# Mixtures of experts computed for the chosen pairs only, in blocks of 128 slots by expert

## Chip, core and metric

The kernel runs on one core of one Trainium2 chip. The metric is the device time of one execution in microseconds. The core's engines are TensorE (PE in the profile, its weight loads PEld), VectorE (DVE), ScalarE (ACT), GpSimd (POOL) and SyncE (SP), which here only issues transfers.

## What is computed

Eight layers run over 8 sequences of 256 tokens with 128 channels, all in float32; after each, `x = layernorm(x + layer(x))`. Four of them are attention-like (a complex scan, causal attention, local attention over a window of 32, attention to the 16 best of the last 32 tokens). The other four are: a mixture of 8 experts with 256 hidden columns, a latent attention with a mixture of 8 experts and a shared one with 128 hidden columns, a dynamics layer with its own small experts, and a mixture of 8 experts with 342 hidden columns. Each mixture has this shape; the reference computes every expert for every token, with weights that are zero for all but two:

```
for e in range(E):
    h = silu(x @ Wg[e] + bg[e]) * (x @ W1[e] + b1[e])
    out = out + we[:, e:e + 1] * (h @ W2[e] + b2[e])
```

`we` holds for each token the weights of its two best experts. The first two mixtures have no biases.

## The kernel before

The 8 sequences are 4 chunks of 2 sequences, 512 tokens each, that is 4 tiles of 128 tokens. All four chunks are under way at once. Each goes through nine stages: A (scan), B (mixture 256), C (causal attention), D1 (latent attention), D2 (mixture 128 with the shared expert), E (local attention), F (dynamics), G (attention to the best of 32), H (mixture 342). A number in brackets is the chunk: B(0) is stage B of chunk 0.

Each engine has a generator per stage that yields after every piece of work. `interleave` runs the four chunks' generators in an order that is written out by hand, one digit (the chunk) per piece: the strings of `MERGE`, one for each engine. `BANK_OF` names in the same way the PSUM bank (8 of 128 x 512 float32) that each group of products writes. Memory regions that chunks share (`att`, `ring`, `dyn`) are handed on in the order of `TURNS`; `take` waits for the last user. Semaphores order everything else, one `Signal` per kind of event.

In a mixture, `chunk_turned` transposes the chunk to channels by tokens (`xt`), `by_token` makes the 8 logits of each token, and VectorE picks the two best (`top2`: `MAX8`, `FIND_INDEX8`, comparison with 0 to 7) and makes a dense weight per token and expert (`densify`). Then `experts` runs on each engine: for each expert and each slice of its hidden columns TensorE makes gate and up over all 512 tokens (`whole`, L450), ScalarE the silu of gate into `hid` (L1818 with bias, L1820 without), VectorE multiplies by up (L1192 with bias, L1195 without), TensorE makes the down product per tile of 128 tokens (L485) and VectorE adds it to `x` with the dense weight (L1209). SP loads each expert's weights (`load_expert`, L2338, L2332 and L2334) into a ring of 4 slots, `w_exp`; the addresses are constants and the loads wait only for their slot. Attention's transposes of probabilities stand at L525 (`turn_probs`). After each stage the norm: `statistics` and `normalise` on VectorE, and between them `power` on GpSimd (L2187, L2188). ScalarE's `table` (L1781) loads another function table where the next function needs one.

GpSimd's work is otherwise part of A (L2214, L2219) and scaling of probabilities (L2199, L2202, L2271). It issues no transfer.

Of the kernel before, what the change touches and what calls it, by code (L numbers as in the profile page):

```python
# [9 lines left out]
U32 = mybir.dt.uint32  # L10
AX_X = mybir.AxisListType.X

D = 128
# [8 lines left out]
E8 = 8  # L22
# [5 lines left out]
RING_H, RING_W = 6, 4  # L28
# [27 lines left out]
TICKS = dict(A=9, B=26, C=25, D1=26, D2=19, E=30, F=58, G=20, H=34)  # L56

TURNS = {
# [10 lines left out]
        "0000000100000011200000000003200000000000000000000231111111101000001100111111101010101010111111111111"  # L69
        "0100000111000010300000111111011000000011101010100000010111110011010101110100001012222222122102000020"  # L70
        "2222202202200202222000002022222022222202200200011111111100001112000000011122221112220000011101111122"
        "1202020012033333333233222233333300002222200220322333232300000111120000321300101011313333311111310010"
        "0133333333300222223223333322330222332323203112322111012221122322133323211111111111121333131333331131"
        "3000300000033333333331113300310333113331111111333111222333311331111113222000000000000022000202000000"
        "2222200020000011200101020220021111222111112212222222222222020022221121003333003003000003003000300322"
        "2222222222222202222222233333011311111111113111111111111131111221121211331113223322333133322222233333"
        "3333311113113333223111211111333333333333333311131333333311122213312232322222222233332333333222222222"
        "2222332232222222332322222222222222222222223333333333333333333333333333333333333333333333333333333333"
# [53 lines left out]
def previous_user(region, k, st):  # L132

    turns = TURNS[region]
    i = turns.index((k, st))
    return turns[i - 1] if i and turns[i - 1][0] != k else None


class Signal:


# [8 lines left out]


FFN = {
    "B": (8, 2, 128),
    "D2": (9, 1, 128),
    "H": (8, 3, M3),
}
# [2340 lines left out]
```

## Time and profile before

| | us |
|---|---|
| median of 3 runs (1224.92 to 1227.92) | 1227.08 |
| the profiled execution | 1226.56 |
| its span, first to last instruction | 1224.5 |
| TensorE busy | 1115.4 |
| VectorE busy | 827.1 |
| ScalarE busy | 657.6 |
| GpSimd busy | 219.1 |

The profile is of one execution. Busy time is the time in which at least one instruction of the engine runs, so for TensorE, whose products overlap, it is less than count times mean. A float32 product is recorded as two instructions, a transpose as one. Of the transfers, the profile knows when they were issued and when they landed; the granted clock is the share of full speed that TensorE had.

### The profile page before, as it was taken

How to read it: one execution, taken by the hardware profiler on the slowest of the kernel's cores; microseconds unless marked ns; L12 is line 12 of the kernel's file. 1: busy time of each engine (PE TensorE's matmuls, PEld its weight loads, DVE VectorE, ACT ScalarE, POOL GpSimd, SP SyncE). 2: the span in 40 equal slices, each digit the busy share in tenths (PEclk: the TensorE clock that was granted, in tenths of full speed). 3: DMA queues.
4: the chain of work that ended last, by engine and by line, in shares of the span. 5: the costliest groups of instructions: out<-in, count | busy, mean ns of one | idle time of the engine just before them, and what ended most of it. 6: DMA issues, size and time to landing. Idle time of an engine off the chain costs nothing.

```text
span 1224.5 us, 16730 instructions
## 1 busy us (share of the span) xinstructions
PE 1115.4 (91%) x5800; PEld 629.4 (51%) x5800; DVE 827.1 (68%) x2446; ACT 657.6 (54%) x1028; POOL 219.1 (18%) x251
## 2 busy tenths in 40 slices
PE   0799967799999999999799989999999999999996
PEld 0455544566554455554455555454464553565554
DVE  6987566489577369868486696678584774664534
ACT  0225344555756766677666575668546655542321
POOL 1312042224021214131200150005020000202000
PEclk9899989899989989997899999799999999999999
DMA  7021100121110000001001111001001010111210
GB/s 268 4 73 54 39 14 14 30 68 34 33 48 24 27 14 21 20 27 33 1 14 56 37 37 37 1 18 37 18 28 37 18 37 1 45 36 54 79 56 9
DMA packets 45394, 45.91 MB, mean 37 GB/s; under 512 B 2584, under 2 KB 44192, under 8 KB 45056
## 3 DMA queue, kind: packets, MB, share of 16 engines
q1 hardware_dynamic: 42336, 40.59, 10.9%
q10 hardware_dynamic: 2976, 4.26, 1.0%
q8 instruction: 47, 0.77, 0.2%
q14 instruction: 35, 0.29, 0.1%
HBM read 43.79 MB, written 1.05 MB: 37 GB/s over the span
## 4 chain that ended last, share of the span: by engine, by line
PE 77%; DVE 13%; ACT 4%; DMA 3%; issue 2%; POOL 1%; POOLq 0%; DVEq 0%; ACTq 0%
PE bank L450 32%; PE bank L485 13%; PE bank L757 10%; PE bank L780 5%; ACT L1781 2%; PE bank L457 2%; PE bank L525 2%; PE bank L439 2%; PE bank L747 1%; PE bank L792 1%; PE bank L668 1%; DMA xt<-x_in 1%; DVE x L1209 1%; DMA w_exp<-in_ffn 1%; PE bank L508 1%
## 5 line engine op out<-in xcount | busy, mean ns | idle before, releaser
L450 PE MATMUL bank<-xt,w_exp 128*128 128x512 f32 (+1 forms) x784 | 390.6, 629 | 19.1 <-DMA w_exp<-in_ffn 6.4
L1781 ACT ACT_TABLE_LOAD x186 | 238.6, 1283 | 70.9 <-PE bank L450 41.7
L450 PEld LDWEIGHTS bank<-xt,w_exp 128*128 128x128 f32 (+1 forms) x784 | 134.5, 190 | 193.7 <-issue 117.1
L485 PEld LDWEIGHTS bank<-w_exp,hid 128*128 128x128 f32 (+1 forms) x1568 | 189.3, 196 | 52.2 <-issue 15.8
L485 PE MATMUL bank<-w_exp,hid 128*128 128x128 f32 (+1 forms) x1568 | 199.0, 282 | 5.7 <-DVE hid L1192 4.2
L1209 DVE SCALAR_TENSOR_TENSOR x<-bank,dense,x 128x128 f32<-128x128 f32 x384 | 107.9, 343 | 119.4 <-PE bank L485 103.0
L757 PE MATMUL bank<-picked,w_dyn 128*128 128x512 f32 x320 | 142.9, 596 | 0.0
L1818 ACT ACTIVATE hid<-bank,w_cols 114x512 f32<-114x512 f32 x96 | 65.2, 687 | 114.6 <-PE bank L450 114.0
L2187 POOL TENSOR_SCALAR rstd<-mv 128x4 f32<-128x4 f32 x32 | 7.0, 218 | 552.6 <-DVE mv L1075 552.4
L1820 ACT ACTIVATE hid<-bank 128x512 f32<-128x512 f32 x100 | 57.5, 597 | 85.1 <-PE bank L450 84.7
L757 PEld LDWEIGHTS bank<-picked,w_dyn 128*128 128x128 f32 x320 | 59.1, 190 | 74.8 <-issue 74.7
L2271 POOL TENSOR_TENSOR att<-att,lsm 128x512 f32<-128x512 f32 x64 | 67.8, 1075 | 140.7 <-DVE lsm L1415 130.1
L1192 DVE SCALAR_TENSOR_TENSOR hid<-bank,w_cols,hid 114x512 f32<-114x512 f32 x96 | 70.3, 745 | 27.4 <-PE bank L450 21.1
L1195 DVE TENSOR_TENSOR hid<-bank,hid 128x512 f32<-128x512 f32 x100 | 66.7, 681 | 17.9 <-ACT hid L1820 14.6
L525 PE MATMUL bank<-w_const,att 128*128 128x128 f32 x304 | 45.2, 283 | 12.0 <-DVE hid L1195 3.6
L1844 ACT COPY att<-bank 128x512 f32<-128x512 f32 (+1 forms) x80 | 41.1, 581 | 20.9 <-PE bank L525 20.9
L525 PEld LDWEIGHTS bank<-w_const,att 128*128 128x128 f32 x304 | 35.7, 145 | 30.8 <-issue 12.7
L780 PE MATMUL bank<-xt,w_dyn 128*128 128x512 f32 (+2 forms) x96 | 49.8, 617 | 1.1 <-DVE xt L1531 1.0
L1555 DVE TENSOR_TENSOR picked<-dyn,bank 128x512 f32<-128x512 f32 x64 | 39.5, 679 | 10.3 <-PE bank L450 10.3
L2202 POOL TENSOR_TENSOR att<-att,rowsum 128x512 f32<-128x512 f32 x32 | 32.8, 1051 | 74.5 <-DVE rowsum L1250 74.5
L1793 ACT ACTIVATE xt<-bank 128x512 f32<-128x512 f32 x24 | 14.3, 594 | 58.3 <-PE bank L439 58.3
L1085 DVE TENSOR_SCALAR x<-x,mv,rstd 128x128 f32<-128x128 f32 x112 | 32.5, 353 | 14.3 <-POOL rstd L2188 14.2
(288 smaller groups left out, 1515.9 us busy)
## 6 DMA issues: line engine op xcount, KB each, us to landing
w_exp<-in_ffn SPq DMA_DIRECT2D x68, 192.0 KB, 3.2
w_exp<-in_ffn SPq DMA_DIRECT2D x32, 384.0 KB, 3.5
w_exp<-in_ffn SPq DMA_DIRECT2D x32, 342.0 KB, 3.1
w_dyn<-in_dyn ACTq DMA_DIRECT2D x1, 1636.0 KB, 12.1
w_const<-in_const SPq DMA_DIRECT2D x1, 1274.0 KB, 11.7
xt<-x_in SPq DMA_DIRECT2D x4, 256.0 KB, 15.4
out<-x ACTq DMA_DIRECT2D x4, 256.0 KB, 2.3
att<-in_stage SPq DMA_DIRECT2D x1, 512.0 KB, 5.2
```

The costliest lines, as they stand in the source:

```text
L450: nc.tensor.matmul(seqs(bk[0:rows, :]) if len(rhs.shape) == 3 else bk[0:rows, :], lhsT, rhs, start=True, stop=True).then_inc(S[k % STREAMS ...
L485: last = nc.tensor.matmul(bk[:, t * 128:(t + 1) * 128], hid[0:rows, (e * nf + f) % RING_H, t * 128:(t + 1) * 128], ffn_w(k, st, "down", e, ...
L525: last = nc.tensor.transpose(bk[:, o:o + 128], a(u)[:, i * 128:(i + 1) * 128], ident)
L757: last = nc.tensor.matmul(bk[:], part("dyn", "ex_w2")[:, h * 384 + at:h * 384 + at + 128], picked[:, 2 * h + t - 1, :], start=False, stop= ...
L780: last = nc.tensor.matmul(seqs(bk[0:rows, :]), lhs, src, start=(half == 0), stop=(half == len(use) - 1))
L1192: V.scalar_tensor_tensor(o, u, col("b1", j, rows), o, ALU.add, ALU.mult).then_inc(X.hidden.s, 1)
L1195: V.tensor_tensor(o, u, o, ALU.mult).then_inc(X.hidden.s, 1)
L1209: last = V.scalar_tensor_tensor(x[:, s, t, :], bk[:, t * 128:(t + 1) * 128], dense[:, s, t, ex:ex + 1], x[:, s, t, :], ALU.mult, ALU.add)
L1781: A.preload_act_table_set(name)
L1818: A.activation(dst, src, ACT.Silu, bias=col("bg", j, rows)).then_inc(X.silu.s, 1)
L1820: A.activation(dst, src, ACT.Silu).then_inc(X.silu.s, 1)
L2271: G.tensor_tensor(v, v, spread(lsm[:, u, row, :], 2, 64), op).then_inc(done, 1)
```

## The change

Each mixture is computed only for the 1024 pairs of token and chosen expert of a chunk. The pairs are put in order of expert, each expert's begin at a multiple of 128, and 15 blocks of 128 slots hold them in every case. The steps:

- VectorE adds the one-hot choices (`count_in`), TensorE makes counts and ranks from them with a triangle of ones (`counts`), VectorE works out each pair's slot (`place`, into `pos`) and each block's expert (`name_blocks`, into `block_expert`; in H also each block's biases, `bias_x`).
- GpSimd scatters the token rows with 8 indirect transfers of 128 rows to a buffer in device memory (`scatter`, `x_slots`, two buffers in turn). SP loads them back in groups of 3 blocks (`load_slots`), TensorE transposes each block, ScalarE copies the group (`xt_group`).
- SP reads each block's expert into a register (`expert_of`) and loads gate and up weights and down weights into two rings of 4 (`load_gu`, `load_dn`). TensorE makes gate, up and down for the block's 128 slots (`products`), ScalarE and VectorE silu and product as before on 128 columns per slice (256 in B, 384 in D2's groups).
- ScalarE copies a group's results (`y_group`), SP stores them (`store_slots`, `y_slots`), GpSimd gathers each token's two rows with 8 indirect transfers (`gather`), VectorE adds them with their two weights (`combine`). The shared expert of D2 runs over all tokens with weights of its own in place (`w_shared`).
- Before GpSimd's first work in stage A it waits for six new transfers that fill `x_slots` (twice 1921 rows of 512 bytes, from the input in device memory) and one row of each `y_slots`.
- `MERGE`, `BANK_OF` and `TURNS` are written anew, and SP has an order of its own. The mixtures share no region any more; D2(0) comes after B(3). In F, the router's first values go to `nx`, so that `dyn` is taken later. `hid` has 4 slots of 384 columns in place of 6 of 512.

The core of the diff, without the new orders:

```diff
+NB, GROUP = 15, 3
+GROUPS = NB // GROUP
+MIX = {"B": (2, 128), "D2": (1, 128), "H": (3, M3)}
...
+            def counts(k, st):
+                bk = begin(k, (st, "counts"), (T.placed, (k, st, "read")))
+                pe.wait_ge(T.placed.s, T.placed.at(k, st, "counted"))
+                nc.tensor.matmul(bk[:, 0:40], part("const", "ones"), routing(s)[:, 40:80], start=True, stop=False)
+                nc.tensor.matmul(bk[:, 8:40], tri[:], routing(s)[:, 0:32], start=False, stop=True).then_inc(T.filled, 1)
...
+            def products(k, st, u, half, bk, at):
+                nf, rows = MIX[st]
+                for n, j in enumerate(blocks_of(st, u)):
+                    if half == 0:
+                        pe.wait_ge(*gu_landing(k, st, j))
+                    g = j // GROUP
+                    for f in range(nf):
+                        o = at + (n * nf + f) * 128
+                        c = (j % GROUP) * 128
+                        last = nc.tensor.matmul(bk[0:rows, o:o + 128], w_gate_up(k, st, j, half, f),
+                                                xt_group[:, group_slot(k, st, g), c:c + 128], start=True, stop=True)
+                return last
...
-                    for t in range(TILES):
-                        for f in range(nf):
-                            last = nc.tensor.matmul(bk[:, t * 128:(t + 1) * 128],
-                                                    hid[0:rows, (e * nf + f) % RING_H, t * 128:(t + 1) * 128],
-                                                    ffn_w(k, st, "down", e, f), start=(f == 0), stop=(f == nf - 1))
...
+            def combine(k, st):
+                w2 = small1(s, S_W, 2)
+                dve.wait_ge(T.gathered, 128 * (list(MIX).index(st) + 1))
+                for t in range(TILES):
+                    last = V.scalar_tensor_tensor(x[:, s, t, :], nx[:, s, t, :], w2[:, t, 0:1], x[:, s, t, :],
+                                                  ALU.mult, ALU.add)
+                step(last)
+                for t in range(TILES):
+                    last = V.scalar_tensor_tensor(x[:, s, t, :], second(s, t), w2[:, t, 1:2], x[:, s, t, :],
+                                                  ALU.mult, ALU.add)
...
+            for n in range(2):
+                act.dma_start(x_slots[n], x_in.rearrange("g d b t -> (g d b t)")[0:(1 + SLOTS) * D].rearrange(
+                    "(r d) -> r d", d=D)).then_inc(slots_set, 16)
...
+            pool.wait_ge(slots_set, 32 + 16 * STREAMS)
...
+            def scatter(k, st):
+                if n >= 2:
+                    for g in (GROUPS - 2, GROUPS - 1):
+                        pool.wait_ge(*group_landing(x_landed, *MIXES[n - 2], g))
+                pool.wait_ge(T.placed.s, T.placed.at(k, st, "pos"))
+                for i in range(2 * TILES):
+                    G.indirect_dma_start(x_slots[n % 2][:], bass.IndirectOffsetOnAxis(ap=pos[:, s, i:i + 1], axis=0),
+                                         src[:, s, i // 2, :], None).then_inc(T.scattered, 16)
+                    if i % 2:
+                        yield
+            def gather(k, st):
+                for g in (GROUPS - 2, GROUPS - 1):
+                    pool.wait_ge(*group_landing(y_stored, k, st, g))
+                for i in range(2 * TILES):
+                    dst = second(s, i // 2) if i % 2 else nx[:, s, i // 2, :]
+                    G.indirect_dma_start(dst, None, y_slots[s][:],
+                                         bass.IndirectOffsetOnAxis(ap=pos[:, s, i:i + 1], axis=0)).then_inc(T.gathered, 16)
...
+            def expert_of(k, j):
+                return sp.value_load(block_expert[0:1, k % STREAMS, j:j + 1], min_val=0, max_val=E8 - 1)
+            def load_gu(k, st, i):
+                if i == 0:
+                    sp.wait_ge(T.placed.s, T.placed.at(k, st, "blk"))
+                if n >= RING_W:
+                    q, u, v = GU_LOADS[n - RING_W]
+                    sp.wait_ge(*spent(q, u, unit_of(u, GU_ITEMS[u][v][-1])))
+                m = nf * rows
+                for j in GU_ITEMS[st][i]:
+                    e = expert_of(k, j)
+                    at = (j - GU_ITEMS[st][i][0]) * 256
+                    sp.dma_start(w_gu[:, n % RING_W, at:at + 2 * m].rearrange("p (g n) -> p g n", g=2),
+                                 sources[st][:, 0:2, bass.ds(e * m + (128 if st == "D2" else 0), m)]).then_inc(
+                                     gu_landed[n % RING_W], 16)
```

## Rows read from the trace of the kernel before

**Rows 1.** The page, part 1: busy time, share of the span, instructions.
```profile
PE 1115.4 (91%) x5800; PEld 629.4 (51%) x5800; DVE 827.1 (68%) x2446; ACT 657.6 (54%) x1028; POOL 219.1 (18%) x251
```

**Rows 2.** Windows: stretch, length, busy and instructions per engine, PEclk, DMA share, GB/s.
```profile
0.00:36.00 36.00, 3.53 (x15) 2.81 (x15) 25.07 (x90) 2.08 (x3) 8.04 (x13) 1.00 0.66 228
36.00:200.00 164.00, 143.31 (x727) 87.33 (x726) 118.70 (x411) 68.54 (x147) 39.76 (x53) 0.96 0.11 34
200.00:1000.00 800.00, 757.34 (x4157) 421.56 (x4158) 565.11 (x1588) 505.81 (x769) 153.29 (x172) 0.95 0.10 29
1000.00:1215.00 215.00, 209.32 (x892) 116.12 (x890) 114.06 (x342) 81.12 (x111) 16.83 (x12) 0.99 0.14 41
```

**Rows 3.** Timeline (start, length): first product, GpSimd's first in A, last down products.
```profile
27.29 1.09 PE L439 MATMUL bank<-w_const,att 128*128 128x128 f32 x4 [27.29 <-DVE att L1280]
...
19.83 1.70 POOL L2214 TENSOR_TENSOR att<-xt,inject 128x512 f32<-128x512 f32 x1 [13.92 <-DMA xt<-x_in]
...
1212.92 2.92 PE L485 MATMUL bank<-w_exp,hid 114*128 114x128 f32 x24 [1.97 <-DVE hid L1192]
```

**Rows 4.** Groups by line, TensorE: busy us, mean ns, idle before.
```profile
L450 PE MATMUL bank<-xt,w_exp 128*128 128x512 f32 (+1 forms) x784 | 390.6, 629 | 19.1 <-DMA w_exp<-in_ffn 6.4 <-ACT att L1835 4.9 <-DVE hid L1192 2.5
...
L485 PE MATMUL bank<-w_exp,hid 128*128 128x128 f32 (+1 forms) x1568 | 199.0, 282 | 5.7 <-DVE hid L1192 4.2 <-DVE att L1412 0.5 <-DVE att L1431 0.3
...
L525 PE MATMUL bank<-w_const,att 128*128 128x128 f32 x304 | 45.2, 283 | 12.0 <-DVE hid L1195 3.6 <-POOL att L2202 2.4 <-ACT hid L1820 1.9
```

**Rows 5.** Groups by line and form, VectorE and ScalarE.
```profile
L1781 ACT ACT_TABLE_LOAD x186 | 238.6, 1283 | 70.9 <-PE bank L450 41.7 <-PE bank L780 13.5 <-DVE negmax L1242 8.1
...
L1209 DVE SCALAR_TENSOR_TENSOR x<-bank,dense,x 128x128 f32<-128x128 f32 x384 | 107.9, 343 | 119.4 <-PE bank L485 103.0 <-issue 14.4 <-DVE x L1680 0.9
...
L1192 DVE SCALAR_TENSOR_TENSOR hid<-bank,w_cols,hid 114x512 f32<-114x512 f32 x96 | 70.3, 745 | 27.4 <-PE bank L450 21.1 <-ACT hid L1818 5.7
L1195 DVE TENSOR_TENSOR hid<-bank,hid 128x512 f32<-128x512 f32 x100 | 66.7, 681 | 17.9 <-ACT hid L1820 14.6 <-PE bank L450 2.7
L1818 ACT ACTIVATE hid<-bank,w_cols 114x512 f32<-114x512 f32 x96 | 65.2, 687 | 114.6 <-PE bank L450 114.0
L1820 ACT ACTIVATE hid<-bank 128x512 f32<-128x512 f32 x100 | 57.5, 597 | 85.1 <-PE bank L450 84.7
...
L1844 ACT COPY att<-bank 128x384 f32<-128x384 f32 x16 | 7.3, 483 | 6.7 <-PE bank L525 6.7
...
L1835 ACT ACTIVATE att<-att,negmax 128x128 f32<-128x128 f32 (+1 forms) x32 | 14.2, 443 | 2.4 <-DVE negmax L1239 2.0
```

**Rows 6.** Groups by line, GpSimd.
```profile
L2271 POOL TENSOR_TENSOR att<-att,lsm 128x512 f32<-128x512 f32 x64 | 67.8, 1075 | 140.7 <-DVE lsm L1415 130.1 <-DVE lsm L1423 10.1
L2188 POOL TENSOR_TENSOR rstd<-rstd,expo 128x4 f32<-128x4 f32 x40 | 41.4, 1034 | 3.3
...
L2187 POOL TENSOR_SCALAR rstd<-mv 128x4 f32<-128x4 f32 x32 | 7.0, 218 | 552.6 <-DVE mv L1075 552.4
```

**Rows 7.** Transfers by line: count, KB each, median us from issue to landing.
```profile
w_exp<-in_ffn SPq DMA_DIRECT2D x68, 192.0 KB, 3.2
...
out<-x ACTq DMA_DIRECT2D x4, 256.0 KB, 2.3
```

**Rows 8.** The load of weights in B and D2, SP's time to issue (ns, min/median/max).
```profile
L2338 SPq DMA_DIRECT2D w_exp<-in_ffn x68: 539/540/6406, 7.1 to 660.6; - x68
```

**Rows 9.** Windows in the head (columns as in rows 2).
```profile
10.00:15.00 5.00, 0.00 (x0) 0.00 (x0) 4.61 (x24) 0.00 (x0) 0.00 (x0) 1.00 1.00 377
15.00:20.00 5.00, 0.00 (x0) 0.00 (x0) 2.94 (x10) 0.00 (x0) 0.17 (x1) 1.00 1.07 313
```

**Rows 10.** Timeline of B(0): logits, reading them, end of the one-hot choice.
```profile
34.65 1.84 PE L457 MATMUL bank<-w_lat,xt 128*128 128x8 f32 x8 [0.84 <-ACT xt L1793]
...
40.05 0.18 DVE L1144 COPY small<-bank 128x32 f32<-128x32 f32 x1
...
41.57 0.29 DVE L1125 TENSOR_TENSOR oh<-w_const,small 128x32 f32<-128x32 f32 x2
```

More of the change, by code:

```diff
@@ new lines, in stage_h @@
+                chunk_turned(k, "H", "g", x)
+                yield
+                bk = begin(k, ("H", "cent"), (T.routed, (k, "cent")))
+                nc.tensor.matmul(bk[:, 0:E8], part("const", "ones"), sc[:, C_SQ:C_SQ + E8],
+                                 start=True, stop=True).then_inc(T.filled, 1)
+                yield
+                pe.wait_ge(T.xt_ready.s, T.xt_ready.at(k, "H"))
+                by_token(k, ("H", "logits"), xt_tile(s), part("rows", "centroid"), E8, (T.logits, (k, "H")))
@@ L974, in _ @@
+                pe.wait_ge(T.turned.s, T.turned.at(k, "H", "weights"))
+                pe.wait_ge(landed["b2"], 16)
+                for t in range(TILES):
+                    last = nc.tensor.matmul(bk[:, t * 128:(t + 1) * 128], flat(s)[0:E8, t * 128:(t + 1) * 128],
+                                            w_b2[:], start=True, stop=True)
+                last.then_inc(T.filled, 1)
+                yield
+                yield from mixture_steps(k, "H")
             for name in ("cols", "const"):
@@ L1326, in stage_c @@
+                yield
             def stage_c(k):
@@ new lines, in stage_d2 @@
+                lg = read_logits(k, "D2")
+                step(V.tensor_tensor(lg, lg, spread(part("rows", "e_bias"), 1, TILES), ALU.add))
+                softmax_in(k, lg)
+                yield
+                top = top2(s, softmax_out(k, "D2"))
+                yield
+                count_in(k, "D2")
+                yield
+                pair_softmax_in(k, top)
+                yield
+                for u in ("sh0", "sh1"):
+                    h = hid_unit(k, "D2", u)
+                    dve.wait_ge(T.filled, T.full(k, "D2", "up", u))
+                    dve.wait_ge(T.silu.s, T.silu.at(k, "D2", u))
+                    V.tensor_tensor(h, T.bank(k, "D2", "up", u)[:, 256:512], h, ALU.mult).then_inc(T.hidden.s, 1)
+                    yield
@@ new lines, in stage_h @@
+                for t in range(TILES):
+                    last = V.tensor_tensor_reduce(nx[:, s, t, :], x[:, s, t, :], x[:, s, t, :],
+                                                  1.0, 0.0, ALU.mult, ALU.add, sm(s, S_A, TILES)[:, t:t + 1])
+                step(last)
+                yield
+                dve.wait_ge(T.filled, T.full(k, "H", "cent"))
+                V.tensor_copy(sm(s, S_B2, E8), T.bank(k, "H", "cent")[:, 0:E8]).then_inc(T.routed.s, 1)
+                lg = read_logits(k, "H")
@@ new lines, in stage_h @@
+                yield
+                dve.wait_ge(T.filled, T.full(k, "H", "b2"))
+                dve.wait_ge(T.filled, T.full(k, "H", "turn", 0))
+                V.tensor_tensor(x[:, s], tiles(T.bank(k, "H", "b2")[:]), x[:, s], ALU.add).then_inc(T.resid.s, 1)
+                dve.wait_ge(T.resid.s, T.resid.at(k, "H"))
+                yield
+                yield from mixture_steps(k, "H")
+                combine(k, "H")
+                yield
+                statistics(k, "h", x_tiles(s))
@@ L2225, in stage_b @@
             def stage_b(k):
-                for i in range(TICKS["B"]):
-                    if i == 24:
-                        power(k, "b")
-                        yield
+                yield from scatter(k, "B")
+                yield from gather(k, "B")
+                power(k, "b")
+                yield
             def stage_c(k):
```

978 lines of the change are left out of this document (613 added, 365 removed), and 6 rows, old and new, of the table TURNS.

## The prediction

> **What bounds the kernel now.** First the page: TensorE is busy 91% of the span and nearly evenly, VectorE 68%, ScalarE 54%, GpSimd 18% [rows 1]. Then the windows: of its 109 idle us 53 lie in the first 200; from 200 to 1000 us it works 757.3 of 800 us, from 1000 to 1215 us 209.3 of 215 [rows 2]. So TensorE's work bounds the kernel, after a head of 27 us in which it has none [rows 3]. Then the groups by line: the mixtures' gate and up products (L450 with w_exp) are 390.6 us, the down products (L485) 199.0 us [rows 4]. Together 589.6 us, over half of TensorE's time, and it is this that the change rewrites. Each token goes through all 8 experts though only 2 count.
>
> **TensorE, removed and added.** A float32 product has two records here. Of 512 columns, 392 gate and up products cost 390.6 / 392 = 0.996 us each; of 128 columns with weights of their own, 784 down products cost 199.0 / 784 = 0.254 us each [rows 4]. So narrow products cost nearly the same per column (1.98 against 1.95 ns), and cutting blocks of 128 slots is not dearer. After, a chunk has 15 blocks with 4 + 2 narrow products in B, 2 + 1 in D2, 6 + 3 in H: 15 x 18 = 270, for 4 chunks 1080 x 0.254 = 274 us. The shared expert: per chunk 4 products of 256 columns and 4 of 128, 1536 columns x 1.95 ns = 3.0, in all 12 us. New transposes: 15 per mixture, 180 x 0.149 (45.2 / 304, one record each [rows 4]) = 27 us. The counts take under 3 us. New sum 316, so TensorE loses 589.6 - 316 = 273 us and has 1115 - 273 = 842 us.
>
> **The other engines.** VectorE loses the mixing into x (107.9), the products in hid (70.3 + 66.7) and the adding of dense weights (some 7): 252 us [rows 5]. It gains 60 products of 256 columns at about 0.41 (between 0.34 for 128 and 0.68 for 512 columns), 20 of 384 at 0.55 and 8 of 256, 180 of 128 with a bias at 0.343, 96 combining ones at 0.343, and per mixture some 18 small routing operations at 0.2 plus H's block biases (5 of about 0.6): 25 + 14 + 62 + 33 + 55 + 3 = 192. It ends at 767 us. ScalarE loses 65.2 + 57.5 and gains 60 x 0.4, 28 x 0.5, 180 x 0.4 (nearest: 0.443 for 128 columns) and 120 copies of 384 columns at 0.483: 168, so about 703 us if the 186 table loads stay as many (238.6 us [rows 5]; 150 to 260 of them would be -46 to +95 us, beside TensorE as long as ScalarE stays under the span). GpSimd gains 192 indirect transfers, 8 to scatter and 8 to gather in each of 12 mixtures. No row shows one. Below: 0.22 us, its cheapest row of this size; above: 3.2 us, as if each took as long as a load of 192 KB to land; I take 1.03, its row for an operation that on 4 columns costs about what others cost on 512, so one whose price is its start, as that of 128 offsets should be [rows 6, 7]. 198 us, so 417 us.
>
> **SP's queue.** Today SP issues 132 load instructions; then 40 per mixture, 480, and 360 of them read the block's expert from SBUF into a register first. All stand in one order, and a load waits for its slot, a store for ScalarE's copy, so whatever is behind waits too: the next weights, hence TensorE. An issue takes 0.54 us [rows 8]. The register read v has no row: below 0 (hidden under the issue), above 3.2 us (a round trip like a load); I take 0.54, a second step of SP's own kind. A block then needs 2 x (0.54 + v) + 2/3 x 0.5 = 1.41 + 2v = 2.5 us of SP. TensorE's block needs 6 x 0.254 + 0.15 = 1.67 us in B, 9 x 0.254 + 0.15 = 2.43 in H. **So wherever mixtures stand alone, SP takes TensorE's place as the bound.** The Trainium skill ("DMA: Bandwidth & Descriptors", Latency and other measured facts) gives a load into registers a floor of about 600 ns; with it the sum below would be some 14 us higher, and no row of this trace shows it. Transfers themselves: an H block moves 546 KB of weights and 128 KB of slots in and out per block, 0.67 MB / 2.5 us = 270 GB/s, B 0.39 + 0.13 MB, 210 GB/s; the head shows 313 to 377 GB/s with all engines full [rows 9]. Close, but not the bound.
>
> **Head.** Chunk 0's logits end at 36.5 us and its first gate product starts right behind [rows 10]. After, it waits: top two to 42 (the VectorE rows from 40.05 to 41.86 [rows 10]), count and PE count 1.8, places 8 x 0.2 plus a cast = 2, scatter 8 x 1.03 + 2.3 (the shortest landing [rows 7]) = 10.5, group load 3.2, turn and copy 1.1: 61 us.
> **B of four chunks.** In TensorE's new order, what stands up to B(3)'s last down product is the four B's (108 us), C(0), C(1) and D1(0) (38) and the beginnings of C(2), D1(1) and D2(0) (13); I count each step with a product's duration above, which over the whole order gives 936 for 842, so all such sums are taken times 0.9: 143 us. 60 blocks of SP give 60 x 2.5 = 150. SP decides: 61 + 150 = 211 us.
> **Middle,** from there to where H(0) goes on in one piece with H(1), H(2), H(3) behind: 842 - 143 - 150 = 549 us of TensorE's work (the 150: 151 for the four H's without H(0)'s first blocks and 17 for the ends of F(3), G(2) and G(3), times 0.9). Today's share in the middle is 94.7%, in the thinner stretch from 36 to 200 us 87.4% [rows 2]. The chain of a mixture has grown: from counts to first turn 2 + 10.5 + 3.2 = 16 us, and the order puts 10 and 13 us of other work there in D2(1), D2(0), 15 in H(3), 20 to 64 in the rest; from last down to the next stage copy 0.5, store 2.8, gather 10.5, combining 2.7 and the norm 4, 21 us, covered by 12 us in D2(0), 20 to 27 in the B's, 32 to 37 in the other D2's. VectorE grows from 0.74 to 0.91 of TensorE's busy time, ScalarE from 0.59 to 0.83. So I take 88%, near the thin stretch: 624 us, and 549 / 0.946 = 580 as the good end.
> **Tail:** 60 H blocks, 150 us of TensorE and 150 of SP; as both must fit, 160 us. **End:** from the last down to the end today 8.7 us [rows 3]; plus copy, store, gather and combining less the mixing it replaces: 24 us.
> Sum 61 + 150 + 624 + 160 + 24 = 1019 us of span. The profiled execution's own time is 2.1 us above its span (1226.56 to 1224.5) and 0.5 under the median: 1021 us. Only 206 of the 273 us come through, because SP, the longer chains and the thin head and tail take their part.
>
> **The rivals.**
> *Everything is covered* (15%): v near 0 and a middle at 94.6%. 61 + 143 + 580 + 152 + 22 = 958, us 960. For it: nobody but TensorE is over 80%. Against: four ordered queues that wait for each other, where today only TensorE matters.
> *The slots are filled by one DMA engine* (20%). GpSimd now waits, ahead of all its work, for two copies of 1921 rows of 512 bytes from memory to memory. Spread over 16 engines, 1.97 MB cost 5 us at 377 GB/s [rows 9], less than the 1.5 MB of weights no longer loaded there, so my sum has nothing for it. On one engine they run at 377 / 16 = 23.6 GB/s: 83 us, plus that engine's part of the rest (228 GB/s x 36 us [rows 2] / 16 at that rate, 22 us). GpSimd's first operation, at 19.8 us [rows 3], would start at 107, and with it stage A: +87, so 1108 us. The Trainium skill (the same page, Why a DMA increments its semaphore by 16 and not by 1) says that a transfer is spread over the largest number up to 16 that divides its slowest dimension; 1921 is 17 x 113, so by that rule one engine. No row here shows such a transfer, and whether the two contiguous sides keep that form can't be read from the text.
> *Slow indirect transfers* (12%): at 3.2 us GpSimd has 833 us and every scatter and gather is 17 us longer. Head +17, end +17, and in the middle and at H(3), where 10 to 27 us cover 16 to 21, about 60: 1115 us. GpSimd's powers for the norms of the other chunks stand behind it in one order.
> *SP reads slowly* (8%), the slower side: B and tail are both 60 blocks of SP. The sum is 61 + 624 + 24 + 120 x (1.41 + 2v) = 878 + 240v; it passes 1227 at v = 1.45 us. With v at 2.3, the shortest landing of any transfer [rows 7], 1430 us. Against it: the value lies in on-chip memory, not behind a DMA. For it: 360 reads, each between two issues, nothing beside them.
> *Two of these troubles together* (4%): the filling, slow transfers and half of a slow read add up to 87 + 94 + 100 us or more, past 1227.
>
> **How the numbers follow.** Forecast 1021 us at 41% (950 to 1075 with v from 0.2 to 0.8 and a middle of 85 to 94%); covered 15%, one engine 20%, slow indirect 12%, slow SP 8%, several together 4%. Low end 945, inside the covered case's lower edge; the high end takes in one engine and slow transfers, also partly together, 1175. That leaves out the slow SP case, the combinations and the edges, some 18%. Faster by over 0.3% (about what a measurement can tell here) 87%, within 0.3% 1%, slower 12%: the last two cases.
>
> **What would show it.** TensorE busy 842 us, 5% either way; if it is over 900 the narrow products are dearer than the old down rows (a lower granted clock in a thinner stream would do that). First group transposed at 61 us; at 100 or later it is the filling, with GpSimd idle until then on DMA. SP's register read shows as the gap between two issues of weights, 0.54 us; GpSimd's transfers as their distance in a scatter, 1.03. In the B stretch and the tail TensorE's idle time should stand against loads of weights. If the middle is under 85%, look for norms (rstd) that wait behind a gather.

## The result

The changed kernel takes 1219.81 us (median of 20 runs, 1213.34 to 1228.17) against 1227.3 us before (20 runs): a ratio of 0.9942, 95% interval 0.9924 to 0.996. The forecast was 1021 us, range 945 to 1175. So the kernel is faster by about what can be measured, and not by 17%; the range missed it by 45 us.

One finding of the experiments is needed to read this number: in one group of later runs (group 4 below, on a chip that no other group used) the changed kernel took 1158.09 us, and a certain kind of wait that the profile below has is absent there. The kernel before stays at 1225 to 1228 us in all groups.

The page of the profiled execution (span 1220.5 us), the lines that answer to [rows 1]:

```profile
PE 949.9 (78%) x5900; PEld 658.2 (54%) x5900; DVE 760.2 (62%) x2435; ACT 613.5 (50%) x1170; POOL 402.9 (33%) x443
PE   0286587885664758888999899899999999878781
DVE  6774344464464478556776686867866686475441
PEclk9997687897777968698989899888978899889786
```

TensorE lost 165 us of work (1115.4 to 949.9) and gained 162 us of idle time (109 to 270.6). Its clock row is full of 6, 7 and 8, where the kernel before has this one:

```profile
PEclk9899989899989989997899999799999999999999
```

By the windows (columns: length, busy us of TensorE, its weight loads, VectorE, ScalarE and GpSimd, granted clock, DMA share, GB/s), cut where the forecast cut: head, B of the four chunks, middle, tail, end; they answer to [rows 2]:

```profile
0.00:62.60 62.60, 9.14 (x37) 7.39 (x37) 43.08 (x161) 4.22 (x6) 21.20 (x25) 1.00 0.49 172
62.60:285.00 222.40, 169.84 (x1156) 146.73 (x1156) 114.43 (x458) 94.54 (x221) 86.65 (x108) 0.85 0.52 151
285.00:990.20 705.20, 601.77 (x3444) 347.78 (x3445) 479.40 (x1322) 420.88 (x696) 228.74 (x247) 0.85 0.15 44
990.20:1195.00 204.80, 169.17 (x1265) 156.29 (x1263) 118.68 (x476) 93.34 (x246) 57.29 (x54) 0.90 0.69 192
1195.00:1220.50 25.50, 0.00 (x0) 0.00 (x0) 4.64 (x20) 0.48 (x1) 8.99 (x10) 0.59 0.14 39
```

The groups by line (busy us, mean ns, then idle time ahead of them and what ended most of it): gate and up products, down products, transposes, and GpSimd's scatters and gathers. The first two answer to [rows 4]:

```profile
L655 PE MATMUL bank<-xt_group,w_gu 128*128 128x128 f32 (+1 forms) x1440 | 214.4, 302 | 31.2 <-issue 10.7 <-ACT hid L2128 4.9 <-ACT xt_group L2150 4.5
L701 PE MATMUL bank<-w_dn,hid 128*128 128x128 f32 (+1 forms) x720 | 115.2, 298 | 22.5 <-DVE hid L1479 9.3 <-ACT hid L2128 5.6 <-ACT early L2163 3.9
L670 PE MATMUL bank<-w_const,x_group 128*128 128x128 f32 x180 | 34.8, 312 | 34.7 <-DMA x_group<-x_slots 19.0 <-issue 8.6 <-ACT att L2179 3.4
L2561 POOL DMA_INDIRECT x_slots<-x,pos x64 | 63.8, 997 | 80.1 <-DVE pos L1431 54.7 <-issue 25.2 <-DVE x L1302 0.3
L2574 POOL DMA_INDIRECT nx<-y_slots,pos x48 | 47.1, 981 | 89.3 <-DMA y_slots<-early 77.3 <-issue 11.7
```

A product has two records, so it costs 214.4 / 720 = 0.298 and 115.2 / 360 = 0.320 us, where the sum had 0.254.

Then a part of the timeline that has no like before: a burst of gathers (start, us, engine, line, operation, and idle time ahead of it; lines are left out at the dots):

```profile
118.83 1.06 PE L655 MATMUL bank<-xt_group,w_gu 128*128 128x128 f32 x8
...
119.86 0.38 ACT L2130 ACTIVATE hid<-bank 128x256 f32<-128x256 f32 x1
...
120.83 0.71 PE L701 MATMUL bank<-w_dn,hid 128*128 128x128 f32 x4
122.01 0.94 POOL L2574 DMA_INDIRECT nx<-y_slots,pos  x1 [0.30 <-issue]
123.26 0.95 POOL L2574 DMA_INDIRECT xt<-y_slots,pos  x1 [0.30 <-issue]
124.51 0.95 POOL L2574 DMA_INDIRECT nx<-y_slots,pos  x1 [0.30 <-issue]
...
126.64 0.38 ACT L2130 ACTIVATE hid<-bank 128x256 f32<-128x256 f32 x1 [6.39 <-remote]
127.12 0.43 DVE L1479 TENSOR_TENSOR hid<-bank,hid 128x256 f32<-128x256 f32 x1 [6.34 <-remote]
...
127.60 0.90 PE L670 MATMUL bank<-w_const,x_group 128*128 128x128 f32 x3 [6.06 <-issue]
```

TensorE's eight records at 118.83 make gate and up of one block and end at 119.9. ScalarE, which needs only them, starts on that block at 126.64 (its work at 119.86 is for the block before): the semaphore that they raise is recorded as raised at 126.55. VectorE and TensorE stand behind it; GpSimd alone goes on, a gather every 1.25 us. The waits table books such waits under "remote", since no instruction of the time ended them. It has 27 of them, 118.7 us summed over the engines, and the trace has some 50 updates by TensorE that come more than 0.6 us late, up to 10.8, nearly all of them while GpSimd issues a row of indirect transfers; the trace of before has none of either. They are called late updates below.

### The profile page after: what moved, and what is told of

Same layout as the page of the kernel before. It is cut to its first block, busy times and chain, and to the rows that moved or that the text cites. A ratio compares the mean times of both kernels' runs of the same rounds, so it can differ in the third digit from the quotient of the medians.

```text
span 1220.5 us, 19615 instructions
## 1 busy us (share of the span) xinstructions
PE 949.9 (78%) x5900; PEld 658.2 (54%) x5900; DVE 760.2 (62%) x2435; ACT 613.5 (50%) x1170; POOL 402.9 (33%) x443
## 4 chain that ended last, share of the span: by engine, by line
PE 51%; DVE 15%; ACT 8%; issue 8%; POOL 5%; SPq 5%; DMA 4%; another core or an unknown queue 3%; ACTq 1%; POOLq 0%; DVEq 0%
PE bank L655 10%; PE bank L973 9%; PE bank L597 7%; PE bank L701 5%; PE bank L996 4%; ACT L2090 2%; SPq L2701 2%; PE bank L740 2%; PE bank L604 2%; POOL x_slots L2561 2%; DMA x_group<-x_slots 2%; PE bank L586 2%; PE bank L670 1%; PE bank L963 1%
## 5 line engine op out<-in xcount | busy, mean ns | idle before, releaser
L655 PE MATMUL bank<-xt_group,w_gu 128*128 128x128 f32 (+1 forms) x1440 | 214.4, 302 | 31.2 <-issue 10.7
L655 PEld LDWEIGHTS bank<-xt_group,w_gu 128*128 128x128 f32 (+1 forms) x1440 | 197.1, 209 | 41.1 <-issue 17.4
L701 PE MATMUL bank<-w_dn,hid 128*128 128x128 f32 (+1 forms) x720 | 115.2, 298 | 22.5 <-DVE hid L1479 9.3
L701 PEld LDWEIGHTS bank<-w_dn,hid 128*128 128x128 f32 (+1 forms) x720 | 101.8, 211 | 29.2 <-DVE hid L1479 11.3
L2561 POOL DMA_INDIRECT x_slots<-x,pos x64 | 63.8, 997 | 80.1 <-DVE pos L1431 54.7
L1475 DVE SCALAR_TENSOR_TENSOR hid<-bank,early,hid 114x128 f32<-114x128 f32 x180 | 51.4, 345 | 55.6 <-ACT hid L2128 23.8
L2128 ACT ACTIVATE hid<-bank,early 114x128 f32<-114x128 f32 x180 | 53.3, 369 | 55.1 <-PE bank L655 37.9
L2574 POOL DMA_INDIRECT nx<-y_slots,pos x48 | 47.1, 981 | 89.3 <-DMA y_slots<-early 77.3
L2130 ACT ACTIVATE hid<-bank 128x256 f32<-128x256 f32 (+1 forms) x88 | 35.7, 412 | 58.5 <-PE bank L655 29.8
L2574 POOL DMA_INDIRECT xt<-y_slots,pos x48 | 45.6, 951 | 15.3 <-issue 15.3
```

Source lines behind the costliest of these rows:

```text
L655: last = nc.tensor.matmul(bk[0:rows, o:o + 128], w_gate_up(k, st, j, half, f), xt_group[:, group_slot(k, st, g), c:c + 128], start=True, s ...
L701: last = nc.tensor.matmul(down[:, o:o + 128], h[:, at:at + 128], w_down(k, st, j, f), start=(f == 0), stop=(f == nf - 1))
L1475: last = V.scalar_tensor_tensor(h[:, c], bk[0:rows, c], bias_of(k, u, 1)[0:rows, f:f + 1], h[:, c], ALU.add, ALU.mult)
L2128: last = A.activation(h[:, c], bk[0:M3, c], ACT.Silu, bias=bias_of(k, u, 0)[0:M3, f:f + 1])
L2561: G.indirect_dma_start(x_slots[n % 2][:], bass.IndirectOffsetOnAxis(ap=pos[:, s, i:i + 1], axis=0), src[:, s, i // 2, :], None).then_inc(T ...
L2574: G.indirect_dma_start(dst, None, y_slots[s][:], bass.IndirectOffsetOnAxis(ap=pos[:, s, i:i + 1], axis=0)).then_inc(T.gathered, 16)
```

## The experiments

Five groups of runs, each on one chip with the kernel before beside them: groups 1 to 3 on one chip, 4 and 5 on two others. Waits on "remote", summed over the engines of each profile, sort them: none in groups 1, 2 and 4, 85 to 114 us in 3 and 5. The changed kernel itself ran in groups 3, 4 and 5 only.

**Group 1: what GpSimd's transfers and SP's reads cost.** Added to the kernel before are 24 bursts, from six places in the code, of which one is shown (the other two kernels have a plain transfer in the loop, or 16 multiplications in place of it):

```diff
+            def burst():
+                if bursts[0]:
+                    pool.wait_ge(moved, 128 * bursts[0])
+                bursts[0] += 1
+                for i in range(8):
+                    at = bass.IndirectOffsetOnAxis(ap=pos[:, i:i + 1], axis=0)
+                    G.indirect_dma_start(rows_out[:], at, junk[:], None).then_inc(moved, 16)
...
                         power(k, "a")
+                        burst()
```

> The kernel before, whole, with 24 bursts of 8 indirect transfers of 128 rows added on GpSimd that nobody uses: 12 behind the norms of A and D1 and the distances of H, 12 ahead of the norms of B, D2 and H, about where the change has its scatters and gathers. Theory 1 (the transfers themselves hold up TensorE: in the changed kernel its completions arrive up to 10 us late inside such bursts and nowhere else, and the whole core stands still some 45 us there): 2 to 3 us for each burst, so +48 to +72 us, 1275 to 1300 us, TensorE idle between its products with nobody to name, granted clock down from 0.96 to about 0.93. Theory 2 (they are harmless beside TensorE, and the changed kernel's idle time is its chains of waits): within 5 us of 1227, clock 0.96. GpSimd gets 24 x 10.2 = 245 us more to do, 18% to 38% busy; if that alone delays the norms, the run with plain work on GpSimd shows the same.

> As the run with indirect transfers, but each of the 192 is a plain transfer of the same 64 KB from the same tile to 128 rows in a row, issued by GpSimd. If it is the lists of addresses (indirect) that hold TensorE up, this is within 5 us of 1227; if it is any transfer issued by GpSimd, it is as slow as the indirect ones (theory 1: 1275 to 1300 us); theory 2: 1227 for both.

> As the run with indirect transfers, but in place of each burst GpSimd multiplies 16 times 128 x 256 elements, some 10 us: the control for GpSimd being late for the norms. Theory 1: it is the transfers, not GpSimd's time, so 1227 to 1240 us. Rival: GpSimd's lateness makes all of the loss, then this run has the same time as the indirect one.

Measured: 1319.66 us (ratio 1.0753, interval 1.0732 to 1.0775), 1260.71 (1.0272, 1.025 to 1.0293) and 1362.22 (1.1096, 1.1052 to 1.114). No wait on "remote" in any. Multiplying costs more than the indirect transfers, and its 24 bursts hold GpSimd longer (290.8 us against 189.3 + 56.8). So theory 1 falls here, and so does theory 2: no update by TensorE is late beside the transfers, and yet they cost 92 us. The reading that is left is that GpSimd is late for other work. VectorE's waits for norms, first before, then with indirect transfers, then with multiplications (from each kernel's table of waits: us in total, times, the longest):

```profile
DVE x L1085 <- POOL rstd L2188: 16.9, 18, 1.5
```
```profile
DVE x L1089 <- POOL rstd L2206: 69.1, 20, 21.4
```
```profile
DVE x L1086 <- POOL rstd L2195: 79.0, 20, 24.7
```

With plain transfers, which hold GpSimd 104 us, it is 37.2 us. Where GpSimd's 10 us stand ahead of a norm that the next stage needs, they are on the path. These waits have grown by 52 us; how the 92 us divide is not shown. And the multiplications are no clean control: with them VectorE is busy 865.1 us for 827.1 before, with the indirect transfers 825.4.

Fixed experts, in the changed kernel (most blocks then use the weights of another expert than they should):

```diff
-                return sp.value_load(block_expert[0:1, k % STREAMS, j:j + 1], min_val=0, max_val=E8 - 1)
+                return j % E8
```

> The changed kernel with the block's expert fixed as its number modulo 8: SP reads no register from SBUF, the 360 loads keep their sizes and waits (most blocks use another expert's weights than they should). The change's trace has a read at 0.27 + 0.15 us plus gaps, some 0.5 of 1.15 us between two loads of weights. If SP's rate bounds the B stretch and the tail as forecast, 120 blocks save 2 x 0.5 us each where SP is alone the bound, 60 to 120 us: 1100 to 1160 us. If what is missing lies in TensorE's clock and in waits that SP has no part in, under 20 us: 1200 to 1219.

Measured: 1135.87 us. Set against 1220 that would confirm SP as the bound, and for two groups I took it so. But the changed kernel had not run in this group. Against the time that it has without late updates (1158 us, group 4, another chip) it is 22 us.

**Group 2: reads and transfers apart.** The read kept but not used; the read done once for both loads of a block; no transfers by GpSimd, with and without reads:

```diff
+            experts = {}
+
             def expert_of(k, st, j):
+                if (k, st, j) in experts:
+                    return experts.pop((k, st, j))
```
```diff
-                    G.indirect_dma_start(x_slots[n % 2][:], bass.IndirectOffsetOnAxis(ap=pos[:, s, i:i + 1], axis=0),
-                                         src[:, s, i // 2, :], None).then_inc(T.scattered, 16)
+                    pool.sem_inc(T.scattered, 1)
...
-                    G.indirect_dma_start(dst, None, y_slots[s][:],
-                                         bass.IndirectOffsetOnAxis(ap=pos[:, s, i:i + 1], axis=0)).then_inc(T.gathered, 16)
+                    G.memset(dst, 0.0).then_inc(T.gathered, 1)
```

> The changed kernel with all 360 register reads on SP kept, but the load that follows takes block number modulo 8 as its expert, a fixed address (most blocks use another expert's weights than they should). It parts the two things that the run with fixed experts took away (1136 against 1220 us). If the read itself makes the loss: 1205 to 1225 us, and TensorE's completions arrive late in GpSimd's bursts as in the changed kernel. If it is the load with an address from a register: 1136 to 1150 us. If it is only SP's time: a read is some 0.45 us and the address arithmetic 0.15, so three quarters of the 84 us come back, about 1200.

> The changed kernel, whole and right, with each block's expert read once and the register used for both of the block's loads: 180 reads in place of 360, all addresses from registers as before. If reads make the loss in proportion: 1170 to 1185 us. If what counts is whether any read stands inside a burst of GpSimd: 1195 to 1215. If it is the address from a register: 1210 to 1220.

> The changed kernel without GpSimd's 192 indirect transfers: a scatter only raises its semaphore, a gather sets its 8 destinations to zero (about 0.2 us each), so no token is moved; reads, loads of weights and of slots, products and waits stay. What goes is 24 x 10.2 us of GpSimd, of which the chains scatter to first turn and last down to next stage hold 10 us each. Theory reads-with-bursts (SP's reads and GpSimd's transfers together hold up TensorE's completions): no late completions are left, 1100 us or less, and fixed experts gain nothing more on top. Theory SP-rate: the late completions stay or SP is the bound in B and the tail, and fixed experts gain 50 us or more on top of this too.

> As the run without indirect transfers, and with the block's expert fixed as its number modulo 8, so no register reads either: the fourth corner of the square (changed kernel 1220, fixed experts 1136, no transfers, neither). Theory reads-with-bursts: within 15 us of the run without transfers alone. Theory SP-rate: 50 to 90 us under it, as with transfers. This is also what the fewer columns and the clock alone leave: with TensorE's 830 us at the full clock and 88% of it, about 1000 to 1050 us.

Measured: 1144.43, 1138.41 (ratio 0.9299, interval 0.9265 to 0.9334), 1118.24 and 1090.67 us. All four have no wait on "remote". The expectations on the 84 us have no object if the changed kernel, had it run here, would have taken its 1158 us and not 1220; that is likely and not shown. What stands without it: set against half the reads or unused ones, taking away the transfers gives 20 to 26 us (1138 or 1144 to 1118), without reads 45 us (1136 to 1091, across groups 1 and 2, both without "remote"); fixed experts without transfers give 28 us. Against the changed kernel at 1158 us of group 4, moving tokens costs 40 us and the reads beside it 28 more, so even with both for nothing 1091 us are left, 70 over the forecast.

**Group 3: the changed kernel again.** With itself: the same number of reads but half of them unused (the second hit on a block reads again and drops the value), reads without the check of bounds, and TensorE filled ahead of the norms:

```diff
+                bk = begin(k, (st, "xt"), (S[s].xt_ready, (k, st)))
+                for _ in range(2):
+                    nc.tensor.matmul(bk[:], ident, part("const", "window"), start=True, stop=True)
                 pe.wait_ge(S[s].normed.s, S[s].normed.at(k, norm))
```

> The changed kernel itself once more, beside the three others of this group and with a profile of its own: 1213 to 1228 us. It shows whether TensorE's late completions inside GpSimd's bursts (up to 10 us in the first profile, none in the profile of before and in those with fixed experts, with reads alone, with each expert read once, and without transfers) belong to the program or to one execution: if to the program, stretches of 2 to 5 us with TensorE, VectorE and ScalarE all idle stand again at about 121, 143, 181, 250, 372, 1070 and 1135 us.

> As the run in which each block's expert is read once (1138 us), but where the second load reuses the register, SP reads the value again into a register that nobody uses: the same 360 reads, bound checks, address calculations and loads as in the changed kernel, 1536 program rows of SP in place of 1176, only that half of the loads don't wait for a value just read. If SP's amount of work or of instructions makes the 84 us: 1205 to 1225 us. If it is that a load's address waits for its own read: 1138 to 1160 us.

> The changed kernel, whole and right, without the check of bounds that follows each of the 360 reads; reads, address calculations and loads as they are, 1176 program rows of SP in place of 1536. A check costs 0.02 to 0.03 us in the trace, up to 0.70 in a burst. If the number of SP's instructions is what counts: about 1138 us, the same as with half the reads. If the reads themselves count: 1200 to 1220 us.

> The kernel with each expert read once (1138 us), and in each of the 32 stages that begin with turning the activations, ahead of the wait for the norm, TensorE multiplies twice 512 columns into the bank that it fills next (overwritten, no part of the result): some 2 us each at the full clock, 65 us in all, of which what stands in waits costs nothing. If TensorE's clock falls in just these waits (about 70 us of waiting for norms in that kernel): the time at 1.2 GHz falls from 259 us to under 200 and the rest of TensorE's work from 921 to under 900 us, total 1120 to 1140 us. If the clock falls elsewhere, or the filling only adds: 1150 to 1190 us, and the time at 1.2 GHz stays near 259.

Measured: 1222.19, 1218.1, 1200.75 and 1219.97 us, all with "remote" (88, 96, 90 and 114 us). The last one broke the series: SP's work in it is that of the single reads, which had none in group 2 on the same chip. Within the group, leaving out 360 checks of bounds gives 21 us (0.9791, 0.976 to 0.9821, against 0.9954), unused reads nothing beyond the scatter.

**Group 4: place or timing.** 361 empty instructions ahead of SP's loads; 20 of them in place of a second read:

> The changed kernel with 361 instructions that do nothing ahead of SP's first mixture load, executed in the first 48 us when SP has nothing to do: everything behind them on SP stands elsewhere in memory, work and timing stay. If the late completions hang on where SP's program lies: a fair chance that they are gone and the time is 1140 to 1150 us. If on work and timing: 1213 to 1228 us, late completions as before.

> The same 361 empty instructions in the kernel that reads each block's expert once (1138 us, none late). Place of the program: it may come out at 1210 to 1220 us. Work and timing: 1137 to 1145 us.

> The kernel that reads each expert once, and where the second load would read again, SP executes 20 empty instructions, about as long as a read (0.4 us): 3600 more instructions for SP, no more reads. If SP's pace or its number of instructions brings the late completions: 1200 us or more. If it is the read itself, with its path to the tile in SBUF: 1138 to 1150 us.

Measured: 1158.09 (0.9444, 0.9395 to 0.9493), 1141.84 and 1144.08 us, two runs each, none with "remote". But the empty instructions are not in the program that ran: the first trace has the changed kernel's 19615 instructions, the second the single reads' 19075, engine by engine as many; the third has 144 more on SP, of 3600. So the first is taken for the changed kernel and the second for the single reads, and none of the three tests its theory. What the first shows is more: the same program has two times. The first line of its page and its stretches B, middle and tail (as above):

```profile
PE 928.7 (80%) x5900; PEld 642.2 (56%) x5900; DVE 762.6 (66%) x2435; ACT 614.0 (53%) x1170; POOL 402.6 (35%) x443
```
```profile
62.10:254.70 192.60, 160.57 (x1156) 137.95 (x1156) 115.33 (x459) 94.68 (x221) 86.95 (x108) 0.91 0.60 175
254.70:950.10 695.40, 597.36 (x3444) 346.18 (x3445) 481.36 (x1322) 421.06 (x696) 228.70 (x247) 0.86 0.15 44
950.10:1129.80 179.70, 161.62 (x1265) 150.76 (x1263) 118.61 (x476) 93.55 (x246) 57.26 (x54) 0.93 0.76 219
```

And the same gathers beside the same B stage, with ScalarE starting 0.1 us after TensorE's records have ended (115.26 + 1.06 us) instead of 6.7:

```profile
115.26 1.06 PE L655 MATMUL bank<-xt_group,w_gu 128*128 128x128 f32 x8
...
115.86 0.95 POOL L2574 DMA_INDIRECT nx<-y_slots,pos  x1 [0.30 <-issue]
...
116.41 0.38 ACT L2130 ACTIVATE hid<-bank 128x256 f32<-128x256 f32 x1 [0.42 <-PE bank L655]
```

**Group 5: side by side.** The changed kernel, the single reads and the filled one, unchanged from groups 2 and 3:

> The changed kernel itself, as the measure of this group of runs: 1155 to 1165 us without late completions of TensorE, or 1213 to 1228 us with some 50 of them. Theory group (the late completions belong to the group of runs): either value. Theory program: 1213 to 1228 us, and the 1158 us of the last group stay unexplained.

> Each block's expert read once, in the same group as the changed kernel itself. Theory group: in a group without late completions 1138 to 1144 us, 1.5% to 2% under the changed kernel there; in one with them 1190 to 1210 us, with late completions too. Theory program: 1138 to 1144 us without late completions while the changed kernel has them at 1220 us.

> The kernel with single reads and two products of 512 columns ahead of each wait for a norm, in the same group. What the filling does to the clock is read against the single reads in this group: if the clock falls in just these waits, the time at 1.2 GHz is 60 us or more below that of the single reads, and the total within 10 us of it; if the filling mostly adds, 1160 to 1180 us in a group without late completions (65 us of products, of which about half stand in waits).

Measured: 1216.96 (0.9919, 0.99 to 0.9937), 1205.51 (0.9829, 0.981 to 0.9847) and 1219.65 us (0.9934, 0.9909 to 0.9958), with 89, 85 and 108 us of "remote". So the single reads have two times as well, from one and the same source: 1138.41 us in group 2 without late updates, 1205.51 here with them. Halving SP's reads does not remove them. Single reads give 11.5 us here and 16 in group 4. For the filling, the pages of the single reads and of the filled kernel (mean granted clock 0.865 over 1204.4 us and 0.867 over 1223.5):

```profile
PE 939.7 (78%) x5900; PEld 652.8 (54%) x5900; DVE 760.9 (63%) x2435; ACT 613.7 (51%) x1170; POOL 403.3 (33%) x443
```
```profile
PE 994.2 (81%) x6028; PEld 671.7 (55%) x6028; DVE 759.1 (62%) x2435; ACT 614.3 (50%) x1170; POOL 403.9 (33%) x443
```

55 us of products cost 14 us of time, so most of it stood in waits, more than the half expected; but the time at 1.2 GHz is 2 x (1 - 0.865) x 1204.4 = 325 us in the one profile and as much in the other. Over the other runs it is 318 to 331 us with single reads and 299 to 308 filled (granted clocks 0.863 to 0.868 and 0.874 to 0.877), some 20 us less where 60 were expected. The clock does not fall because of these waits alone, and the filling is no remedy.

## Why the prediction was wrong

The profiled spans beside the forecast, in us, for the same program in the two conditions:

| | forecast | group 4 | profile above |
|---|---|---|---|
| head | 61 | 62.1 | 62.6 |
| B of four chunks | 150 | 192.6 | 222.4 |
| middle | 624 | 695.4 | 705.2 |
| tail | 160 | 179.7 | 204.8 |
| end | 24 | 25.4 | 25.5 |
| span | 1019 | 1155.2 | 1220.5 |
| TensorE busy | 842 | 928.7 | 949.9 |

**What held.** Head and end within 2 us. VectorE 760 for 767, GpSimd 403 for 417. Filling the slots: the page has the two copies of 960.5 KB at a median of 8.5 us to landing, and GpSimd's first operation in A came at 23 us for 20 before. The rival of one engine (83 us) falls, and with it my reading, from the 1921 rows of this copy, of the Trainium skill's rule ("DMA: Bandwidth & Descriptors", Why a DMA increments its semaphore by 16 and not by 1); how the copy was cut up, no run shows. An indirect transfer takes 0.95 to 1.0 us and 0.30 to the next, 1.25 to 1.3 for the 1.03 taken from [rows 6]; the slow rival (3.2) falls. ScalarE has 613.5 us for 703, mostly since 136 table loads stand where I left 186.

**The term that was mis-sized: TensorE's work.** 842 us were forecast, 928.7 came even in group 4. Of these 87 us, 43 are in the mixtures' products (205.8 + 110.7 = 316.5 for 274), 7 in the transposes (34.5 for 27), 3 in the shared expert (15 for 12), 7 in the counts (10.4 for 3) and 26 in the work that the change doesn't touch: 552 for 526. The numbers of products were right; nearly every kind got dearer, and most of it is the granted clock: 0.959 before, 0.879 in group 4 and 0.860 in the profile above. Two places of the tail in group 4, the same 12 records at the higher and at the lower level, by the timeline:

```profile
1073.06 1.47 PE L655 MATMUL bank<-xt_group,w_gu 128*114 128x128 f32 x12
```
```profile
1092.81 2.88 PE L655 MATMUL bank<-xt_group,w_gu 128*114 128x128 f32 x12 [0.69 <-ACT xt_group L2150]
```

```profile
1071.00:1079.00 8.00, 7.49 (x69) 7.29 (x67) 6.92 (x24) 4.78 (x15) 6.17 (x7) 1.00 0.95 278
1089.00:1097.00 8.00, 5.06 (x23) 4.72 (x24) 2.67 (x8) 1.84 (x5) 1.07 (x1) 0.50 0.81 233
```

A product costs 0.245 us at 2.4 GHz and 0.48 at 1.2. The clock had gone to 1.2 GHz at 1087.9, half a microsecond into a wait of 3.8 us for slots. Time at 1.2 GHz, from the mean clock: 2 x (1 - 0.959) x 1224.5 = 100 us before, 2 x 0.121 x 1155.2 = 280 us in group 4, 342 us in the profile above. TensorE works in 84, 203 and 240 us of them. As its work takes twice as long there, half of that is what the lower level costs (an estimate, as are the next two): 42 us before, of which the 842 carry 32, and 102 in group 4. So some 70 of the 87 us are the clock. The other 17 are not: down products that lie wholly in stretches at 2.4 GHz take 0.292 us in group 4, where before they took 0.250, and the counts are far over their 3 us at either level. I took every duration from a kernel at 0.959. The text had the right suspicion, over 900 us "a lower granted clock in a thinner stream", but kept it as a thing to look for, gave it neither a chance nor a price, and summed 842 us of work into a stream that it itself made thinner (83% busy for 91%). In the terms of its sum, the duration of 0.254 us per narrow product, and with it the 842 us of which B and the middle were made, is the step that failed.

**The busy shares of middle and tail were about right.** Middle: 597.4 of 695.4 us, 85.9% for the 88% taken; with 48 us more work that is the 71 us. Tail: 161.6 of 179.7, 90% for 94%. So the good rival (960 us, a middle at 94.7%) falls too.

**SP is not the bound.** A second step that fails is "wherever mixtures stand alone, SP takes TensorE's place". The price was near (a read 0.27 us for 0.54, its calculation 0.15, an issue 0.35 to 0.41 for 0.54; with the gaps, two weight loads 1.13 us apart for the 1.08), but 180 reads less on SP (81 us of it) give 11.5 to 16 us and 360 less some 22, of 1158; the rival of slow reads (v = 1.45 us and more) falls by far. In group 4 SP itself waits, 38 us in the B stretch and 69 in the tail, mostly for TensorE. In the tail:

```profile
SPq L2749 <- PE bank L670: 31.5, 1, 31.5
SPq L2701 <- PE bank L655: 15.6, 16, 3.2
SPq L2701 <- PE bank L701: 14.4, 10, 6.7
```

B's 192.6 us hold 160.6 us of TensorE's work where the sum had 143 and let SP's 150 decide; the other 32 are waits of many kinds. Those for SP's loads are 12 of them (5.1 for slots, 7.3 for weights), and 9 of the tail's 18, so SP has a part and is not the bound. The Trainium skill's floor of about 600 ns for a register load ("DMA: Bandwidth & Descriptors", Latency and other measured facts) is above what the trace shows for reading a register from SBUF: a median of 0.269 us, and 0.44 with calculation and check.

**What no step had: the late updates.** The changed kernel takes 1158 us without and 1217 to 1222 with them, 60 us or 5%: 30 in B, 10 in the middle, 25 in the tail (65 between the two profiles). With them the time lies beyond the range; without them it is inside, 137 us over the forecast. Of the 65 us, 21 are work that got dearer (949.9 for 928.7) and 44 are idle time.

**Still open.** What delays TensorE's semaphore updates inside GpSimd's bursts. It needs something that the changed kernel has and the kernel before has not, whose time stays at 1227 us in groups 3 and 5 too. It isn't the second read of each expert; whether it needs reads at all is not shown, since the changed kernel without any ran in groups 1 and 2 only. Whether transfers alone bring it was only tried in group 1, and the changed kernel without transfers only in group 2, both without late updates, so neither rules anything out. Nor is it shown what switches it on. Each program that ran in both conditions did so on different chips; groups 1, 2 and 3 share a chip, but no changed program. So it may be the group, the chip, or chip and program together.

Why the clock falls more is told only in part. Ahead of 25 of the 31 stretches at 1.2 GHz in group 4 TensorE had just stood idle for 0.8 us or more, and it is these that have grown, from 50 to 215 us. But there are others, 51 us before and 65 in group 4, ahead of which it had hardly stopped or not at all, as this one:

```profile
581.60:589.60 8.00, 8.00 (x24) 3.25 (x24) 3.01 (x27) 6.69 (x13) 2.95 (x3) 1.00 0.15 41
590.00:603.00 13.00, 13.00 (x24) 4.82 (x23) 12.53 (x36) 8.66 (x12) 5.92 (x7) 0.50 0.12 32
```

No run tests what sets either kind.

## What to carry to other kernels

Removing a quarter of an engine's work from a stream that was nearly full did not remove it at the old price here: take the durations at the clock that the thinner stream will get, and give that a place among the rivals. Moving tokens through memory puts bursts of 10 us on GpSimd, ahead of every norm behind them; count them for all chunks. And before two variants are compared, run the unchanged one in the same group: for two groups I read as an effect of the edit what was, for all that the later groups show, mostly a difference between groups.

The best version here is the changed kernel with each block's expert read once: 0.9829 of the kernel before in one condition, 0.9299 and 0.9312 in the other, and 0.9% to 1.4% under the changed kernel itself.

## What the runs showed of the hardware

- TensorE's semaphore updates came up to 10.8 us late while GpSimd issued indirect transfers (profile above), and in the same profile SP's simplest steps swell: its check of bounds, 18 ns in the median, takes up to 711 ns in the profile above and at most 28 in group 4; its address calculation up to 708 for at most 177 ns. First the profile above, then group 4 (count, then duration in ns: least, median, most):

```profile
L2701 SPq FUSED_REGOPS  x360: 3/152/708, 48.9 to 1189.6; - x180
L2701 SPq SEQ_ASSERT  x360: 2/18/711, 49.1 to 1189.8; - x180
```
```profile
L2701 SPq FUSED_REGOPS  x360: 152/152/177, 48.8 to 1125.1; - x180
L2701 SPq SEQ_ASSERT  x360: 18/18/28, 49.0 to 1125.3; - x180
```

- An indirect transfer of 128 rows of 512 bytes holds GpSimd 1.25 to 1.3 us from start to start, a burst of eight some 10.2 us (group 1: 0.986 us each and 0.30 between two).
- Two copies of 960.5 KB from memory to memory, 1921 rows of 512 bytes, land in 8.5 us (median, profile above).
